# Moving three small reductions on VectorE: strided maximum, strided sum and inverse ahead of the masked score maxima

## What is computed

```
def _L0_attn_ref(x, Wq, Wk, Wv, Wo, lq1, lk1, lq2, lk2):
    ...
    s1 = jnp.where(causal, s1, neg_inf)
    s2 = jnp.where(causal, s2, neg_inf)
    a1 = jax.nn.softmax(s1, axis=-1)
    a2 = jax.nn.softmax(s2, axis=-1)
    o = jnp.einsum('bhst,bthd->bshd', a1, v1) - lam * jnp.einsum('bhst,bthd->bshd', a2, v2)
    ...

def _L0_ffn_ref(x, phi_w, phi_b, expert_w, expert_b):
    ...
    logits = (jnp.einsum('tzd,ed->tze', x, phi_w) + phi_b).reshape(t, z, n, p)
    D = jax.nn.softmax(logits, axis=3)
    C = jax.nn.softmax(logits, axis=2)
    X_tilde = jnp.einsum('tznp,tzd->npd', D, x)
    ...
    Y_tilde = jnp.einsum('npd,ndH->npH', X_tilde, expert_w) + expert_b[:, None, :]
    Y = jnp.einsum('tznp,npH->tzH', C, Y_tilde)
```

## Time and profile before

| | |
|---|---|
| time, median of 3 runs | 1325.7 us (1323.85 to 1325.83) |
| the profiled execution | 1325.38 us, of which the span is 1323.5 us and 1.88 us lie around it |
| instructions | 29570 |
| PE | 95% of the span busy |
| DVE | 87% |
| POOL | 83% |
| ACT | 80% |
| granted PE clock, mean | 0.989 |

### The profile page before, as it was taken

One profiled execution on the slowest core, in us unless ns is written; L12 is line 12 of the kernel. 1 busy time (PEld: TensorE's weight loads), 2 busy tenths in 40 slices (PEclk: granted clock), 3 DMA queues, 4 the chain that ended last, 5 costly groups with the idle time before them and its releaser, 6 DMA issues. The chain is left out here.

```text
span 1323.5 us, 29570 instructions
## 1 busy us (share of the span) xinstructions
PE 1263.7 (95%) x9136; PEld 991.8 (75%) x9136; DVE 1157.0 (87%) x3633; ACT 1062.8 (80%) x3218; POOL 1096.2 (83%) x847
## 2 busy tenths in 40 slices
PE   2999999999999999999999999999999999689998
PEld 2777777777777777777777777777777777478887
DVE  7688999889988998899889988998899988878876
ACT  4688988888888888888888888888898888655554
POOL 1478888888888888888888888888888888789985
PEclk9899999999999999999999999999999999889999
DMA  5111122112111221112211211122111117547783
GB/s 172 54 53 68 71 83 73 71 71 74 58 70 71 76 77 66 70 71 83 73 71 71 72 60 71 69 79 73 68 66 71 71 71 209 154 156 252 250 264 118
DMA packets 105980, 126.31 MB, mean 95 GB/s; under 512 B 20192, under 2 KB 56032, under 8 KB 105696
## 3 DMA queue, kind: packets, MB, share of 16 engines
q1 hardware_dynamic: 102160, 122.97, 27.7%
q10 hardware_dynamic: 3664, 1.44, 0.5%
HBM read 48.89 MB, written 35.65 MB: 64 GB/s over the span
## 5 line engine op out<-in xcount | busy, mean ns | idle before, releaser
L731 ACT ACTIVATE e<-e,neg_max 128x256 f32<-128x256 f32 (+1 forms) x1024 | 451.4, 442 | 58.0 <-DVE neg_max L826 57.3
L826 DVE CUSTOM_DVE_ANT_0 e<-ps_s,mask 128x256 f32<-128x256 f32 (+1 forms) x1024 | 294.1, 351 | 68.0 <-PE ps_s L573 68.0
L1037 POOL TENSOR_TENSOR disp<-logit,gmax 128x512 f32<-128x512 f32 x128 | 134.4, 1050 | 192.5 <-DVE gmax L868 192.5
L1045 POOL TENSOR_TENSOR e<-e,inv 128x1024 f32<-128x1024 f32 x128 | 285.7, 2232 | 0.0
L573 PEld LDWEIGHTS ps_s<-qk 64*128 64x128 f32 x2048 | 172.9, 186 | 49.7 <-issue 45.1
L573 PE MATMUL ps_s<-qk 64*128 64x256 f32 (+1 forms) x2048 | 203.2, 337 | 0.0
L731 ACT ACTIVATION_READ_ACCUMULATOR e<-e,neg_max 128x1 f32 x1024 | 191.2, 187 | 0.0
L556 PEld LDWEIGHTS ps_t<-ident,e 128*128 128x128 f32 x1024 | 119.9, 141 | 68.1 <-issue 64.9
L1073 POOL TENSOR_TENSOR logit<-logit,m_all 128x512 f32<-128x512 f32 x128 | 165.0, 1290 | 0.0
L745 ACT ACTIVATE qk<-ps_t 128x512 f32<-128x512 f32 x126 | 75.3, 598 | 83.8 <-PE ps_t L80 78.7
L617 PE MATMUL ps_o<-pT,v_sb 128*64 128x256 f32 x1024 | 138.8, 392 | 0.0
(11 more groups left out here) (162 smaller groups left out, 3267.2 us busy)
## 6 DMA issues: line engine op xcount, KB each, us to landing
xs<-xT SPq DMA_DIRECT2D x128, 256.0 KB, 2.4
c_scratch<-logit SPq DMA_DIRECT2D x128, 256.0 KB, 2.1
xT<-c_scratch SPq DMA_DIRECT2D x16, 1024.0 KB, 5.4
disp<-c_scratch SPq DMA_DIRECT2D x8, 1024.0 KB, 5.5
logit<-c_scratch SPq DMA_DIRECT2D x8, 1024.0 KB, 6.8
fx<-xT SPq DMA_DIRECT2D x64, 64.0 KB, 1.9
fxn<-xn SPq DMA_DIRECT2D x32, 64.0 KB, 1.9
xT<-in_L_ffn_expert_w SPq DMA_DIRECT2D x4, 512.0 KB, 6.7
```

Source lines behind the costliest of these rows:

```text
L731: ins = nc.scalar.activation(dst, dst, ACT.Exp, bias=neg_max[:, q, c:c + 1], scale=-1.0, accum_out=total[:, q, c:c + 1])
L826: nc.vector.tensor_tensor_reduce(out=dst, in0=part, in1=here, scale=-1.0, scalar=HIGHEST, op0=ALU.add, op1=ALU.min, accum_out=neg_max[:, q ...
L1037: nc.gpsimd.tensor_tensor(by_expert(bank_of(disp, t, jj)), by_expert(bank_of(logit, t, jj)), gmax[:, jj, :].unsqueeze(2).to_broadcast([P, ...
L1045: nc.gpsimd.tensor_tensor(e1[q][:], e1[q][:], inv[:, q, G:2 * G].unsqueeze(2) .to_broadcast([P, G, S]), ALU.mult).then_inc(norm_done, 1)
```

## The change

The three calls move within VectorE's step. No instruction is added or removed, and no other engine's order changes. In the step j = 1 `slot_max_end(it - 1)` and `slot_inverse(it - 3)` now stand between the running maximum and the score maxima; before, they stood behind the score maxima of the step j = 0, a step earlier. `slot_sum(it - 2)` stays in the step j = 3 and moves from behind the score maxima to ahead of them, and ahead of `values_low` and `output_low` too.

```
@@ VectorE, step(it, j, g, kk)
                     next_queries(it, j, 1)
                     slot_max(*back(it, j, 1))
+                    if j == 1:
+                        slot_max_end(it - 1)
+                        if it < ITER + 1:
+                            slot_inverse(it - 3)
+                    elif it < ITER:
+                        slot_sum(it - 2)
                     if live(g + 1, NG) and (kk, j) == (PER - 1, 3):
                         values_low(nc, dve, env, g + 1)
                     if live(g, NG) and (kk, j) == (0, 3) and g > 0:
...
                     bank_max(v, j)
                 if live(g + 1, NG) and (kk, j) == (PER - 1, 2):
                     projections_low(nc, dve, env, g + 1)
-                if j == 0:
-                    slot_max_end(it - 1)
-                if j == 3:
-                    if it < ITER:
-                        slot_sum(it - 2)
-                if j == 0 and it < ITER + 1:
-                    slot_inverse(it - 3)
                 if live(it, NTT):
                     take_logits(it, j)
                 take_slots(it - 1, j)
```

## The result

The changed kernel takes **1319.72 us** in the median of 6 runs (1319.15 to 1322.31), against 1325.07 us for the kernel before (6 runs, 1323.85 to 1325.83). The ratio is 0.9967, with a 95% interval from 0.9957 to 0.9978: 5.35 us faster. The forecast was 1319.8.

What follows compares the result with a forecast made beforehand. PE, 95% busy, was taken as the bound, so DVE's order pays only where PE waits for it. 3.0 + 2.9 − 0.2 = 5.7 us off the profiled 1325.38 gave 1319.7, stated as 1319.8 us; range 1316.5 to 1323.5.

Steps and rivals of the forecast that it cites:

- ordinary steps: Steps without new weights: the moved calls fit into DVE's idle gaps and PE gains nothing, 0 us.
- single exception: The one step, apart from those after `values_low` and `output_low`, where PE was said not to keep its pace.
- The fit into the gaps: Steps j = 1 and 3: 1.40 us into 1.38 idle, 1.06 into 1.11; score maxima slip taken as 0.
- The cover: 14 special steps: L139 and L152 wait for POOL's L1045, so `slot_sum` ahead costs nothing; 0.8 us thick.
- rival 1: 14 special steps: L139 and L152 need 1.98 us wherever they start, maxima come 1.0 us later; 1333.6 us, 9%.
- The first sort of step: Steps after `values_low`: PE's output projection comes 0.43 us earlier, 7 times, 3.0 us.
- the second: Steps after `output_low`: PE's output projection comes earlier, gaining 0.42 us, 7 times, 2.9 us.
- The end: Last odd step with scores: `slot_sum` has no gap and delays the last exponentials; 0.2 us lost, bounds 0 and 0.97.
- PE's wait for L941 would still be there: PE's output projection still waits for L941, while its wait for L861 falls to 1 or 2 us.
- Rival 2: Steps after `values_low` and `output_low`: ACT does not hold L941, which moves by 0.97 us; 1315.3 us, 6%.
- Rival 3: Maxima slip 0.3 us in steps j = 1 and 3, showing in 8 steps behind `projections_high`; 1322.1 us, 9%.
- Rival 4: PE's waits are released by something the trace wrongly puts down to DVE, and stay; 1325.4 us, 4%.

Runs made afterwards that it cites:

- e2: Kernel before with only the strided maximum and the inverse moved, the sum left behind the score maxima of step j = 3; 1325.31 us.
- e10: Changed kernel plus an unused full-size reduction behind the inverse in steps j = 1, kk = 0, 1, 2 only (24 steps); 1319.78 us.
- e3: Changed kernel with the sum behind the low parts of the new weights, right ahead of the score maxima; 1332.64 us.
- e6: Changed kernel plus an unused half-size reduction (256 elements, about 0.5 us) behind the sum in the 14 steps with new weights; 1319.23 us.
- e7: Changed kernel plus an unused full-size reduction (512 elements, about 1.0 us) behind the sum in the 14 steps with new weights; 1336.03 us.
- e5: Kernel before, its three reductions unmoved, with the low parts of new weights behind the score maxima and ahead of the sum; 1320.23 us.
- e11: Changed kernel plus an unused full-size reduction behind the inverse in steps j = 1, kk = 3 only (8 steps); 1326.19 us.
- e1: Kernel before with only the strided sum moved, maximum and inverse left behind the score maxima of step j = 0; 1320.36 us.
- e4: Changed kernel with the low parts of the value and output weights behind the score maxima, ahead of the biased logits; 1311.60 us.
- e12: The kernel of e4 run again on another chip; 1309.31 us, ratio 0.9888 to the kernel before.

## Why the prediction was right

**The place of the loss.** What the change could reach were PE's waits in 14 even steps, behind L861 and then L941; what was written for ordinary steps, a gain of nothing, is e2 and e10. The prediction's "single exception" was not the only one: the steps v = 4 and v = 48 break PE's pace too (8.53 and 10.25 us; 8.50 and 9.94 with the change), but nothing in the sum hangs on it. The fit into the gaps held: with the change the maxima of ordinary odd steps start as far into the step as before, 5.30 us.

**The cover.** The 1.98 us of L139 and L152 are mostly a wait for the end of POOL's instruction. This was the step on which the sign hung, argued from the setup's 0.28 us. Shown by e3 (taken away: 8.7 us more in the main phase than before, where rival 1 had 8.0), e6 and e7 (its thickness: between 0.5 and 1.0 us, as the 0.8 of the prediction).

**The size.** The first sort of step was to gain 0.43 us and gained 0.33; the second 0.42 and gained 0.34. L755 came where it was expected, 2.40 us into the step against 2.38 before, and held L941 (now L947); that ACT is late next is right. What was off by 0.1 is the release behind it: L947 starts 0.61 after L755 and takes 0.69 rather than 0.64 when it comes out of a wait, so that PE follows 0.95 behind its start (719.59 to 720.54) where I had taken 0.90. The sum of the 14 steps was put at 5.9 and measured 4.7 to 5.0. The end was put at −0.2, and the last sum's place costs 0.3. Together that is 4.7 us where 5.7 were forecast. That the time still fell on the forecast is luck: between the two profiled executions, 0.85 us came out of the setup, which no edit touches, and the other runs have no trace that could be divided like this.

**The name on the wait.** I had written that PE's wait for L941 would still be there. It is, but the profile puts it down to ACT's L717. PE follows the end of L947 by 0.26 us (719.59 + 0.69 = 720.28 to 720.54), as it followed that of L941 before (723.69 + 0.64 = 724.33 to 724.59), so the wait is the old one. There are two semaphores, of which the profile names one: the output projection writes into the bank that the first L717 of the step reads, so it waits for that copy too. But the copy is over at 720.04, 0.50 us before PE starts. In the kernel before, where L755 did not hold L941, PE started 0.87 us after that copy and still 0.26 after L941; at every idle wait of this kind in the traces of before, the change, e3 and e5 the distance to the end of DVE's instruction is 0.26, while that to the copy goes from 0.50 to 2.4.

**Rivals.** Rival 1 (9%) was a mechanism that exists, and e3 is what it looks like. Rival 2 is refuted: ACT did hold L941. Rival 3 had the right place (the steps behind `projections_high`) and no occasion here, as the maxima did not slip; e11 shows that a slip there (0.37 us) costs 0.8 us a time rather than its own length, as it has a second link. Rival 4 (4%) is refuted by e1: moving the sum alone takes 5 us off.

## What to carry to other kernels

When an instruction is much longer in the timeline than the same one elsewhere, ask what it waits for inside before calling it work: what is put ahead of it may be free up to a sharp edge, and behind it cost its full length, here 5 us faster against 8 us slower for the same call a few lines apart. Before moving work out of a stall, look up which other engine releases the same instruction: a stall with two holders gives back little when one is removed and the rest when both are. And where one engine is full, whatever feeds the engines that feed it (here the maxima for ACT's exponentials) goes first, the rarely done work last.

## What the runs showed of the hardware that I had not expected

PE's granted clock fell behind the main phase in some executions and not in others, on the same instructions. In e4 (busy by stretches, PEclk is the third number from the right) it stood at 0.50 for a while, the lower level of 1.2 GHz:

```profile
1120.90:1123.00 2.10, 2.10 (x13) 1.34 (x14) 0.78 (x2) 0.52 (x1) 2.10 (x2) 0.50 1.22 212
```

What it costs is seen between e4 and e12, which are the same kernel, from the output projection behind the main phase to the first transpose of `xt_acc` (e4, then e12):

```profile
1119.92:1130.31 10.39, 10.39 (x55) 6.06 (x56) 6.01 (x12) 4.32 (x9) 10.06 (x9) 0.84 0.63 123
```
```profile
1116.23:1125.05 8.82, 8.82 (x55) 5.19 (x56) 6.03 (x12) 4.30 (x8) 8.82 (x8) 1.00 0.85 178
```

The same 55 matmuls take 10.39 us where the clock fell and 8.82 where it stayed at 1.00, as they do in the changed kernel (8.82). PE had been busy for 2.51 of 4.90 us ahead of the fall in e4, and for 2.35 of 4.80 in the changed kernel, where the clock did not fall.

The profiled executions of e4 and e12 are 5.6 us apart: 2.1 us lie in the setup, whose length up to the step v = 2 went from 49.7 to 52.1 us between profiled executions although no edit touched it, 1.6 in DVE's wait for the store, 1.6 in this fall of the clock, and 0.3 behind it; the main phases agree to 0.01. What makes the setup and the store longer or shorter stays open. It is why differences of 1 us in these experiments were read from the main phase and not from medians.
